# Moving the last weighing of a self-attention pair into the next pair's scores

## The chip, the cores and the metric

The kernel runs on one core of a Trainium2 chip. The metric is the device time of one execution in microseconds (us), taken as the median of several runs. The engines are named as the profile names them: PE is TensorE (matmul), PEld its weight loads, DVE is VectorE, ACT is ScalarE, POOL is GpSimd and SP is SyncE.

## What is computed

Two transformer blocks in float32 run over `x` (2 x 512 x 128) with a context of 2 x 154 x 96. The first block is a cross-attention of 16 heads of width 8 with a feed-forward. The second block, in which the change lies, is this:

```python
def _attn(xq, xc, Wq, Wk, Wv, Wo, bo):      # 16 heads of width 64
    q = (xq @ Wq).reshape(B, N, HEADS, D_HEAD)
    k = (xc @ Wk).reshape(B, S, HEADS, D_HEAD)
    v = (xc @ Wv).reshape(B, S, HEADS, D_HEAD)
    attn = softmax(einsum('bnhd,bshd->bhns', q, k) * scale)
    out = einsum('bhns,bshd->bnhd', attn, v).reshape(B, N, HEADS * D_HEAD)
    return out @ Wo + bo

x = _attn(_ln(x, g1, b1), _ln(x, g1, b1), Wq1, Wk1, Wv1, Wo1, bo1) + x   # self
x = _attn(_ln(x, g2, b2), context, Wq2, Wk2, Wv2, Wo2, bo2) + x          # cross
x = _geglu_ff(_ln(x, g3, b3), Wp, bp, Wf, bf) + x
```

## The kernel before

Each engine has one queue of instructions whose order is written out by hand, and semaphores join the queues. Self-attention is done by pairs of heads: 8 pairs for each of the 2 batches make pairs g = 0 to 15 (`NPAIR` = 16), and the cross-attention makes g = 16 to 31. For a self pair the 512 keys are cut into four chunks c = 0 to 3 of 128 keys.

For each self pair g, TensorE does the following, in this order (`attention`, L982 to L998):

1. `all_scores(g)` (L931) calls `scores(g, c)` for the four chunks. One unit of scores is eight matmuls into a two-bank tile `ST`: for each of the two heads three products of queries and keys split in fp32r (L749), and one that subtracts the rows' maxima (L751). A head stands in 64 of the array's 128 rows, so the two heads run side by side. Between them stand two matmuls of the maxima of pair g + 1 (`head_max`, L722), each into a bank `M`.
2. `side_before(g)` (work of other parts, at some g: the feed-forward of the first block at g = 3, values at g = 6 to 11, the spreading of inverse sums at g = 12).
3. `project(g + 2)`, the queries and keys of a later pair (L688 to L706), and `turn_pair(g + 1)`, which turns the maxima (L735).
4. `side_behind(g)` (more of the other parts), and for g >= 1 `denominators(g - 1)`, which is matmuls only for every second pair (L795).
5. `weigh(g, c)` for c = 0 to 3 (L767, matmuls at L780): the exponentials of chunk c, in fp32, as the moving operand against 64 columns of `V` for each head. All four accumulate in the bank `PV`. The profile records each as four matmuls, two for each head, and the heads run side by side in 64 columns each.

There are two `ST` tiles. `claim` (L315) gives them out in turn, and waits until the tile's last user is done: a unit of scores needs the exponential of two units before. There are also two banks `M`; a maximum waits until VectorE has read the one of two before (`maxima`, L1692, reductions at L1698).

ScalarE does for each pair (`attention`, L1371): `weighted(g - 1)` (L1356, a copy of `PV` to `AT` at L1361, which waits for the pair's last weighing), the four `exponentials(g, c)` (L1353) into `PT1[g % 2, c]`, then copies of the side work, then `leading(g + 2)` (L1339). VectorE does the eight reductions of the maxima of g + 1, then `maxima_rows(g + 1)` (L1711), `trailing(g + 2)` (L1685) and its side work. GpSimd adds the four chunks of exponentials (L1196, L1200). `weigh(g, 0)` waits for the copy of the pair before, since `PV` is one bank.

Of the kernel before, what the change touches and what calls it, by code (L numbers as in the profile page):

```python
# [11 lines left out]
TB = N // P  # L12
# [11 lines left out]
NPAIR = B * H // 2  # L24
# [19 lines left out]
def build(nc, a, out):  # L44
    ctx = ExitStack()
    with ctx:
# [138 lines left out]
        def pair(g):  # L185

            ph = self_att if g < NPAIR else cross_att
            return ph, g - ph.first

        def maxima_units(g):  # L190

            return range(TB if g < NPAIR else 2)

        VALUES = {6: (0, TB), 7: (0, TB + 2), 8: (1, 0), 9: (1, 1), 10: (1, 2), 11: (1, 3)}
        SPREADS = {9: (None, 0), 10: (None, 1), 11: (None, 2), 12: (3, None), 18: (None, 0), 19: (1, 2), 20: (3, None),
# [40 lines left out]
        def bank(key):  # L236
            return ST[ring[key]]
# [10 lines left out]
        def head(h):  # L248
            return slice(HD * h, HD * (h + 1))
# [61 lines left out]
        def _(pe):  # L311
# [3 lines left out]
            def claim(key, freed, count):  # L315

                k = len(s_uses)
                if k >= 2:
                    pe.wait_ge(*s_uses[k - 2])
                s_uses.append((freed, count))  # L320
                ring[key] = k % 2
                return ST[k % 2]
# [386 lines left out]
            def project(g):  # L709

                project_leading(g)
                project_trailing(g)

            def head_max(g, c, h):

                ph, i = pair(g)
                if c == 0 and h == 0:
                    pe.wait_ge(ph.hi, i + 1)
                r = R[:, g % 3, 0]
                m = claim_m()  # L720
                for qt, at in ((c, 0),) if ph is self_att else ((2 * c, 0), (2 * c + 1, S)):
                    ins = pe.matmul(m[:, at:at + ph.NK], r[head(h), 0, qt * P:(qt + 1) * P], r[head(h), 1, 0:ph.NK],  # L722
                                    start=True, stop=True)
                ins.then_inc(m_full, 1)
# [12 lines left out]
            def scores(g, c, unit=None, at=(4, 4)):  # L737

                ph, i = pair(g)
                u = claim(("st", g, c), ph.exp, ph.units * i + c + 1)
                k = slice(c * ph.KC, (c + 1) * ph.KC)

                def product(n, h):

                    if n < 3:
                        part_k, part_q = ((0, 0), (0, 1), (1, 0))[n]
                        return pe.matmul(u[0:ph.KC, h, :], R[head(h), g % 3, part_k, 1, k], R[head(h), g % 3, part_q, 0, :],  # L749
                                         start=(n == 0), stop=False)  # L750
                    return pe.matmul(u[0:ph.KC, h, :], onesr[head(h), 0:ph.KC], mrows[head(h), g % 2, :], start=False, stop=True)  # L751

                for n in range(5 if unit is not None else 4):
                    for h in range(2):
                        if unit is not None and n == at[h]:
                            head_max(g + 1, unit, h)
                            continue
                        part = n - (unit is not None and n > at[h])
                        if c == 0 and part == 0:
                            pe.wait_ge(ph.lo, i + 1)  # L760
                        if c == 0 and part == 3:
                            pe.wait_ge(mrow_set, g + 1)
                        ins = product(part, h)
                        if part == 3:
                            ins.then_inc(ph.st, 1)
# [165 lines left out]
            def all_scores(g):  # L931

                ph, i = pair(g)
                if g + 1 == NG:
                    beside = {}
                elif ph is cross_att:
                    beside = {0: (0, (0, 0)), 1: (1, (0, 1))}
                elif g + 1 == NPAIR:
                    beside = {0: (0, (0, 0)), 2: (1, (0, 0))}
                else:  # L940
                    beside = {0: (0, (0, 3)), 1: (1, (1, 3)), 2: (2, (2, 4)), 3: (3, (2, 4))}
                for c in range(ph.units):
                    scores(g, c, *beside.get(c, ()))

            def side_before(g):

                if g == 3:
                    hidden(1)
                if g in VALUES:
                    n, t = VALUES[g]  # L950
                    if n == 1:
                        loaded("wv2")
                    values(n, t)
                if g in SPREADS and SPREADS[g][0] is not None:
                    spread_inverse(g // 8 - 1, SPREADS[g][0])
                if g == 30:
                    turn(3, 0, False)
# [24 lines left out]
            def attention():  # L982

                start_attention()
                for g in range(NG - 1):
                    all_scores(g)
                    side_before(g)
                    if g + 2 < NG:
                        project(g + 2)
                    turn_pair(g + 1)  # L990
                    side_behind(g)
                    if g >= 1:
                        denominators(g - 1)
                    for c in range(pair(g)[0].units):
                        weigh(g, c)
                    if g == 21:
                        turn(2, 1, False)
                all_scores(NG - 1)  # L998
# [217 lines left out]
        def _(act):  # L1216
# [128 lines left out]
            def exponentials(g, c):  # L1345

                ph, i = pair(g)
                act.wait_ge(ph.st, 2 * (ph.units * i + c + 1))
                if g >= 2 and c == 0:
                    old, o = pair(g - 2)  # L1350
                    act.wait_ge(old.pv, o + 1)
                    act.wait_ge(old.sum, o + 1)
                act.activation(PT1[0:ph.KC, g % 2, c], bank(("st", g, c))[0:ph.KC, :, :],  # L1353
                               ACT.Exp, scale=HD ** -0.5).then_inc(ph.exp, 1)

            def weighted(g):  # L1356

                ph, i = pair(g)
                act.wait_ge(ph.pv, i + 1)
                b, j = i // PAIRS, i % PAIRS  # L1360
                act.activation(AT[:, j, b * N:(b + 1) * N], PV[:, :], ACT.Copy).then_inc(ph.pvs, 1)  # L1361
# [9 lines left out]
            def attention():  # L1371

                leading(0)
                values(0, 0)
                values(0, 1)
                exponentials0(7, 0, 1)
                values(0, 2)
                exponentials0(7, 2)
                values(0, 3)
                copy_half0(1, 1)  # L1380
                leading(1)
                for g in range(NG):
                    ph, i = pair(g)
                    if g == 22:
                        scale_features(2, 1)
                    if g >= 1 and g != 22:
                        weighted(g - 1)
                    if g == 2:
                        root(0, 1)
                    for c in range(ph.units):  # L1390
                        exponentials(g, c)
                    if g == 22:
                        weighted(g - 1)
                    if g == 3:
                        act.preload_act_table_set("gelu_and_others")
                        gelus(1)
                    if g in VALUES:
                        values(*VALUES[g])
                    if g == 30:
                        scale_features(3, 0)  # L1400
                    if g + 2 < NG:
                        leading(g + 2)
                    if g == 0:
                        values_bias0(1)
                    if g == 2:
                        scale_features(0, 1)
                    if g == 4:
                        root(1, 1)
                    if g == 5:
                        scale_features(1, 1)  # L1410
                    if g in (6, 7):
                        values(0, VALUES[g][1] + 1)
                    if g in (8, 16, 24):
                        inverse_guess(g // 8 - 1)
                    if g == 12:
                        leading_weights("q2", Wv, w12[:, :])
                    if g == 23:
                        leading_weights("wp", Wk, wp)
                    if g in (12, 20):
                        root(2, g // 8 - 1)  # L1420
                    if g == 13:
                        scale_features(2, 0)
                    if g == 28:
                        root(3, 0)
# [504 lines left out]
```

## Time and profile before

| | us |
|---|---|
| median of 3 runs | 459.2 (458.36 to 459.84) |
| the profiled execution, its own time | 462.21 |
| its span in the trace | 460.4 |
| PE busy | 443.2 (96%) |
| DVE busy | 277.1 (60%) |
| ACT busy | 238.9 (52%) |
| POOL busy | 214.5 (47%) |
| share of PE in the chain that ended last | 86% |

The self pairs take from about 96 us (the scores of pair 0) to about 305 us of the span. The granted TensorE clock is at full speed in that whole stretch. A busy PE is not a PE at its peak, as matmuls are pipelined and the recorded ends of neighbours overlap; how close it is to its bound is read from the starts of its instructions.

### The profile page before, as it was taken

The page shows a single profiled execution, that of the slowest core. Times are in us where ns is not written, and L with a number is a line of the kernel's source. Part 1 is how long each engine was busy: PE and PEld are TensorE (multiplying, and loading weights), DVE is VectorE, ACT ScalarE, POOL GpSimd, SP SyncE. Part 2 cuts the span into 40 slices and gives each one's busy share as a digit, 9 for nine tenths or more (in the row PEclk, how much of TensorE's full clock was granted, in tenths as well). Part 3 has the DMA queues.
Part 4 walks back from the last instruction along what each step waited for, and adds up shares of the span by engine and source line. Part 5 has one row for each costly group of instructions (what it writes and reads, how often), then busy time and mean ns, then how long its engine had stood idle before and what let it go on. Part 6 is the DMA issues. An engine that isn't in the chain of part 4 may idle for free.

```text
span 460.4 us, 7023 instructions
## 1 busy us (share of the span) xinstructions
PE 443.2 (96%) x2758; PEld 263.4 (57%) x2758; DVE 277.1 (60%) x511; ACT 238.9 (52%) x324; POOL 214.5 (47%) x186
## 2 busy tenths in 40 slices
PE   7999999989999999999999999999999999999896
PEld 3654665555655656655545765545575454754696
DVE  1766737576863576467656848447735577553753
ACT  2855465455557366555445526456326665237633
POOL 5488101026884796444566636873326444255010
PEclk9999899899999999999999999999999999999999
DMA  8600000000000100000001010020001000000000
GB/s 251 210 1 2 1 1 0 1 0 1 0 1 1 36 1 0 0 1 1 1 1 46 2 34 1 2 68 1 0 5 44 0 2 2 0 1 1 0 18 30
DMA packets 7985, 8.89 MB, mean 19 GB/s; under 512 B 561, under 2 KB 6129, under 8 KB 7953
## 3 DMA queue, kind: packets, MB, share of 16 engines
q1 hardware_dynamic: 7952, 8.45, 6.0%
q8 instruction: 22, 0.36, 0.3%
q14 instruction: 11, 0.08, 0.1%
HBM read 7.92 MB, written 0.52 MB: 18 GB/s over the span
## 4 chain that ended last, share of the span: by engine, by line
PE 86%; DVE 6%; ACT 4%; issue 2%; DMA 1%; SPq 0%
PE PV L780 18%; PE ST L749 14%; PE M L722 7%; PE ST L751 5%; PE M L828 5%; PE ST L688 5%; PE ST L650 4%; PE DEN L795 3%; ACT PT L1353 2%; PE ST L704 2%; PE ST L668 2%; PE ST L544 2%; PE ST L691 2%; PE M L870 2%; PE ST L366 1%
## 5 line engine op out<-in xcount | busy, mean ns | idle before, releaser
L1196 POOL TENSOR_TENSOR psums<-PT 128x1024 f32<-128x1024 f32 (+1 forms) x32 | 76.1, 2379 | 137.2 <-ACT PT L1353 137.1
L1353 ACT ACTIVATE PT<-ST 128x1024 f32<-128x1024 f32 (+1 forms) x96 | 98.0, 1024 | 39.6 <-PE ST L751 37.9
L1698 DVE TENSOR_REDUCE maxw<-M 128x1 f32<-128x512 f32 x128 | 83.6, 687 | 37.2 <-PE M L722 36.7
L749 PE MATMUL ST<-R 64*128 64x512 f32 (+1 forms) x576 | 105.4, 405 | 0.0
L780 PE MATMUL PV<-PT,V 128*64 128x512 f32 (+1 forms) x384 | 89.5, 601 | 0.0
L1200 POOL TENSOR_TENSOR psums<-psums,PT 128x1024 f32<-128x1024 f32 x32 | 75.9, 2373 | 2.5
L722 PE MATMUL M<-R 64*128 64x512 f32 (+1 forms) x256 | 72.0, 363 | 1.9 <-DVE maxw L1698 0.8
L749 PEld LDWEIGHTS ST<-R 64*128 64x128 f32 (+1 forms) x576 | 57.8, 171 | 14.2 <-ACT PT L1353 8.0
L722 PEld LDWEIGHTS M<-R 64*128 64x128 f32 x256 | 37.2, 185 | 38.1 <-issue 27.1
L780 PEld LDWEIGHTS PV<-PT,V 128*64 128x64 f32 (+1 forms) x384 | 24.7, 136 | 53.9 <-issue 51.5
L1361 ACT ACTIVATE AT<-PV 128x512 f32<-128x512 f32 x32 | 19.1, 598 | 62.5 <-PE PV L780 62.5
L751 PE MATMUL ST<-mrows,onesr 64*128 64x512 f32 (+1 forms) x192 | 47.3, 391 | 0.2 <-DVE mrows L1711 0.2
L1711 DVE TENSOR_TENSOR mrows<-M,cols 128x512 fp32r<-128x512 f32 x32 | 22.1, 691 | 40.5 <-PE M L735 40.5
L1701 DVE TENSOR_REDUCE maxw<-M 128x2 f32<-128x308 f32 x64 | 27.7, 474 | 23.2 <-PE M L722 23.2
L1159 POOL TENSOR_TENSOR X<-X,rows 128x128 f32<-128x128 f32 x24 | 10.4, 461 | 39.3 <-DVE xnT L1611 39.2
L751 PEld LDWEIGHTS ST<-mrows,onesr 64*128 64x128 f32 (+1 forms) x192 | 24.6, 170 | 4.3 <-DVE mrows L1711 0.7
L1339 ACT ACTIVATE R<-ST 128x1024 fp32r<-128x1024 f32 x16 | 16.4, 1024 | 11.2 <-PE ST L706 11.2
L1685 DVE TENSOR_TENSOR R<-ST,R 128x1024 fp32r<-128x1024 f32 x16 | 19.6, 1223 | 4.3 <-ACT R L1339 4.3
L828 PE MATMUL M<-Wo,AT 128*128 128x128 f32 x192 | 21.9, 275 | 0.0
L828 PEld LDWEIGHTS M<-Wo,AT 128*128 128x128 f32 x192 | 21.7, 192 | 0.3
L1556 DVE TENSOR_REDUCE maxw<-ST 128x4 f32<-128x616 f32 x20 | 15.2, 798 | 7.9 <-PE ST L399 7.9
L1311 ACT ACTIVATE lnv<-mv 128x4 f32<-128x4 f32 x7 | 1.4, 204 | 35.4 <-DVE mv L1597 35.4
(257 smaller groups left out, 677.0 us busy)
## 6 DMA issues: line engine op xcount, KB each, us to landing
Wo<-in_wo SPq DMA_DIRECT2D x2, 512.0 KB, 6.4
xnT<-in_xT SPq DMA_DIRECT2D x2, 256.0 KB, 3.4
psums<-in_sel SPq DMA_DIRECT2D x1, 512.0 KB, 5.2
X<-in_x SPq DMA_DIRECT2D x1, 512.0 KB, 6.5
w<-in_w SPq DMA_DIRECT2D x2, 256.0 KB, 6.8
PT<-in_wq SPq DMA_DIRECT2D x1, 512.0 KB, 7.8
PT<-in_wk SPq DMA_DIRECT2D x1, 512.0 KB, 8.1
PT<-in_wv SPq DMA_DIRECT2D x1, 512.0 KB, 7.8
```

The source lines that it names most:

```text
L688: pe.matmul(u[:, 0, :], wq[:, v, k], xh[:, n], start=(v == 0), stop=False)
L722: ins = pe.matmul(m[:, at:at + ph.NK], r[head(h), 0, qt * P:(qt + 1) * P], r[head(h), 1, 0:ph.NK], start=True, stop=True)
L749: return pe.matmul(u[0:ph.KC, h, :], R[head(h), g % 3, part_k, 1, k], R[head(h), g % 3, part_q, 0, :], start=(n == 0), stop=False)
L751: return pe.matmul(u[0:ph.KC, h, :], onesr[head(h), 0:ph.KC], mrows[head(h), g % 2, :], start=False, stop=True)
L780: ins = pe.matmul(PV[head(h), :], V[0:ph.KC, b * ph.NC + c, (2 * j + h) * HD:(2 * j + h + 1) * HD], PT1[0:ph.KC, g % 2, c, h, :], start=(c ...
L828: ins = pe.matmul(u[:, t * P:(t + 1) * P], AT[:, j, (TB * b + t) * P:(TB * b + t + 1) * P], Wo[:, j, :], start=(j == 0), stop=(j == PAIRS ...
L1196: ins = pool.tensor_tensor(s, p[:, 0], p[:, 1], ALU.add)
L1200: ins = pool.tensor_tensor(s, s, p[:, c], ALU.add)
L1353: act.activation(PT1[0:ph.KC, g % 2, c], bank(("st", g, c))[0:ph.KC, :, :], ACT.Exp, scale=HD ** -0.5).then_inc(ph.exp, 1)
L1698: ins = dve.tensor_reduce(maxw[:, g % 2, 0, at:at + 1], m[:, :], AX, ALU.max, negate=True)
L1701: ins = dve.tensor_reduce(maxw[:, g % 2, 0, at:at + 32:16], m[:, 0:2 * S].rearrange("p (t k) -> p t k", t=2), AX, ALU.max, negate=True)
L1711: dve.tensor_tensor(mrows[:, g % 2, :].rearrange("p (t n) -> p t n", t=TB), half_bank(("turn", g))[:, 0:P].unsqueeze(1).to_broadcast([P, T ...
```

## The change

For pairs g = 0 to 14 the weighing of chunk 3 leaves its place behind `weigh(g, 2)` and stands behind unit 1 of the scores of pair g + 1. ScalarE's copy of the pair's values stands behind the exponential of chunk 2 of pair g + 1, where it stood ahead of the exponential of chunk 0. Pair 15 and the cross pairs are left as they were. No instruction is added or taken away. The whole diff:

```diff
@@ -190,6 +190,10 @@
         def maxima_units(g):
 
             return range(TB if g < NPAIR else 2)
+
+        def late_weighing(g):
+
+            return 0 <= g < NPAIR - 1
 
@@ -941,6 +945,8 @@
                 for c in range(ph.units):
                     scores(g, c, *beside.get(c, ()))
+                    if c == 1 and late_weighing(g - 1):
+                        weigh(g - 1, TB - 1)
 
@@ -991,7 +997,7 @@
                     if g >= 1:
                         denominators(g - 1)
-                    for c in range(pair(g)[0].units):
+                    for c in range(pair(g)[0].units - late_weighing(g)):
                         weigh(g, c)
@@ -1383,12 +1389,14 @@
-                    if g >= 1 and g != 22:
+                    if g >= 1 and g != 22 and not late_weighing(g - 1):
                         weighted(g - 1)
                     if g == 2:
                         root(0, 1)
                     for c in range(ph.units):
                         exponentials(g, c)
+                        if c == 2 and late_weighing(g - 1):
+                            weighted(g - 1)
```

## Rows read from the trace of the kernel before

**Rows 1.** The waits: engine, line, releaser: us in total, times, longest

```profile
PEld ST L749 <- ACT PT L1353: 8.0, 28, 0.4
```

**Rows 2.** Timeline of PE, scores of pair 8 (start, us, engine, line)

```profile
199.46 1.03 PE L780 MATMUL PV<-PT,V 128*64 128x512 f32 x4
200.42 0.50 PE L722 MATMUL M<-R 64*128 64x512 f32 x1
...
202.62 0.52 PE L751 MATMUL ST<-mrows,onesr 64*128 64x512 f32 x2
203.00 0.73 PE L749 MATMUL ST<-R 64*128 64x512 f32 x4
...
205.34 0.50 PE L722 MATMUL M<-R 64*128 64x512 f32 x1
205.76 0.65 PE L668 MATMUL ST<-w,ctxT 96*77 96x512 f32 x1
```

**Rows 3.** Timeline of ACT, the same stretch: the copy, the third and fourth exponentials

```profile
200.54 0.60 ACT L1361 ACTIVATE AT<-PV 128x512 f32<-128x512 f32 x1 [2.57 <-PE PV L780]
...
204.45 1.03 ACT L1353 ACTIVATE PT<-ST 128x1024 f32<-128x1024 f32 x1 [0.25 <-PE ST L751]
205.73 1.02 ACT L1353 ACTIVATE PT<-ST 128x1024 f32<-128x1024 f32 x1 [0.26 <-PE ST L751]
```

**Rows 4.** Timeline of DVE, the same stretch: the eight reductions, merged by four

```profile
200.96 2.68 DVE L1698 TENSOR_REDUCE maxw<-M 128x1 f32<-128x512 f32 x4 [3.21 <-PE M L722]
...
203.99 2.57 DVE L1698 TENSOR_REDUCE maxw<-M 128x1 f32<-128x512 f32 x4 [0.35 <-PE M L722]
```

**Rows 5.** The chain in order of time: a matmul; weighings of a self and a cross pair

```profile
114.90 0.23 PE ST L704
...
116.36 3.58 PE PV L780 x16
...
309.92 1.87 PE PV L780 x8
```

**Rows 6.** Timeline of PE: scores' last maximum of pair 6; one weighing

```profile
177.70 0.39 PE L722 MATMUL M<-R 64*128 64x512 f32 x1
183.47 1.08 PE L780 MATMUL PV<-PT,V 128*64 128x512 f32 x4
```

**Rows 7.** Windows: the scores of pairs 2, 6, 9 and 15 (stretch, length, busy)

```profile
119.88:125.22 5.34, 5.34 (x42) 3.74 (x41) 4.55 (x8) 3.99 (x7) 3.86 (x8) 1.00 0.00 0
172.51:178.02 5.51, 5.46 (x42) 3.90 (x41) 5.19 (x8) 3.68 (x4) 1.85 (x2) 1.00 0.00 0
213.71:219.04 5.33, 5.33 (x42) 3.71 (x41) 4.94 (x8) 3.72 (x5) 1.48 (x1) 1.00 0.00 0
295.10:300.22 5.12, 4.67 (x42) 3.33 (x41) 1.73 (x4) 3.62 (x5) 3.23 (x5) 1.00 0.01 3
```

**Rows 8.** Timeline of PE, scores of pair 15: end of the second unit, start of the third

```profile
297.04 0.39 PE L751 MATMUL ST<-mrows,onesr 64*128 64x512 f32 x2
297.66 0.45 PE L722 MATMUL M<-R 64*128 64x154 f32 x4 [0.23 <-ACT PT L1353]
```

**Rows 9.** Timeline of ACT and PE around the feed-forward of pair 3

```profile
138.30 1.28 ACT L1395 ACT_TABLE_LOAD   x1
...
140.91 0.50 PE L688 MATMUL ST<-xh,Wq 128*128 128x512 f32 x1
```

**Rows 10.** Timeline of PE: the projection of pair 12, behind its spreading

```profile
259.42 0.73 PE L688 MATMUL ST<-xh,Wq 128*128 128x512 f32 x2 [0.31 <-ACT PT L1353]
```

**Rows 11.** Timeline of DVE: last work before the reductions in pairs 2 and 9

```profile
119.82 0.17 DVE L1597 TENSOR_SCALAR mv<-mv 128x4 f32<-128x4 f32 x1
...
213.47 0.75 DVE L1726 SCALAR_TENSOR_TENSOR recw<-recw,cols,work 128x512 fp32r<-128x512 f32 x1
```

**Rows 12.** Timeline of POOL and DVE ahead of pair 6

```profile
168.20 4.81 POOL L1200 TENSOR_TENSOR psums<-psums,PT 128x1024 f32<-128x1024 f32 x2
...
170.88 2.68 DVE L1671 TENSOR_TENSOR xl<-xnT,xh 128x512 fp32r<-128x512 f32 x1
```

## The prediction

> **What bounds the kernel now.** I read the page first. PE is busy for 96% of the span and holds 86% of the chain that ended last (the table ahead). Only work taken off PE, or idle time inside it, can shorten this kernel. Next come the waits. The one that touches the scores is short: 8.0 us in 28 waits for an exponential, over the whole program [rows 1]. It is a wait of the weight loads, and a load may wait while the array still works. So the third view is the timeline of PE in one pair, read by the starts. Pair 8 stands for the pattern, since 13 of the 16 self pairs have a score block between 5.33 and 5.37 us long ([rows 7] has pairs 2 and 9; pair 6 takes 5.51, pair 15 5.12, pair 0 more).
>
> In pair 8 the block runs from 200.42 to 205.76 [rows 2]. Its second unit ends with L751 at 202.62 + 0.52 = 203.14, and the third unit starts at 203.00. No time is lost there: the change puts the weighing into a place where PE already works through. The block's end has two bounds. The third exponential ends at 204.45 + 1.03 = 205.48 and frees the tile for the next user [rows 3]. The four reductions run from 203.99 in steps of 2.57 / 4 = 0.64, so the second of them ends at about 205.27, and only then can the last maximum start, at 205.34 [rows 2, 4]. The next work follows at 205.76. VectorE therefore paces the end of the block, counted from the start of the third unit: 205.76 - 203.00 = 2.76 us.
>
> **What the change removes.** Four weighings take 3.58 us, two take 1.87 [rows 5], so one takes (3.58 - 1.87) / 2 = 0.86 us at the end of a row of them. Fifteen go: 15 x 0.86 = 12.9 us off PE.
>
> **What it adds.** The same weighing, alone between two units of scores, costs more than 0.86. Wherever PE passes from the scores (64 rows of the array for each head) to a matmul over all rows, or back, the next start comes 0.07 us before the recorded end of the last one, and not earlier: 199.46 + 1.03 = 200.49 against 200.42; 205.34 + 0.50 = 205.84 against 205.76 [rows 2]; 177.70 + 0.39 = 178.09 against 178.02 [rows 6, 7]. Within a shape, matmuls follow each other every 0.23 us [rows 5] while a record lasts 0.39 [rows 6]. So a pass drains what is under way. At the new place L751 ends at 203.14, and the weighing can start at 203.07. A single weighing lasts 1.08 from its start to its recorded end [rows 6], so the scores go on 1.01 later, at 204.08. That is 204.08 - 203.00 = 1.08 us later than now.
>
> The Trainium skill says under TensorEngine Tiling (Array Packing), Key Properties, that changing the tiling mode, and not just the tile, drains the TensorE. The change has two mode changes more for each pair, and the trace agrees with that rule (0.39 to 0.50 us of the last record, less 0.07, in place of 0.23). A reader who took the weighing as 0.86 wherever it stands would get 0.22 less for each pair.
>
> From the third unit on all is paced from that unit's start: its maxima, their reductions, the last maximum 2.34 later, the next work 2.76 later. The wait for the second exponential in front of the fourth unit goes, but the last maximum waits for the same reduction as before, so this gives nothing back. The third exponential would end 203.00 + 1.08 + 2.48 = 206.56, before the block's new end at 205.76 + 1.08 = 206.84. The price is 1.08 in each block of pairs 1 to 14: 15.1 us. In pair 15 the cross maxima are short; its third unit starts at 297.66 after a wait of 0.23 for the exponential [rows 8]. The second unit ends at 297.04 + 0.39 = 297.43, so the scores go on at 297.36 + 1.01 = 298.37, 0.71 later; this block ends by its third exponential, so 0.71 stays.
>
> **ScalarE's copy.** It takes 0.60 [rows 3] and leaves a place where ACT idles (2.57 us of waiting in front of it), and where nothing waited for it: gain nothing. At the new place it stands between the third exponential and the fourth. In pair 8 the third ends at 206.56, the copy at 207.16, so the fourth ends at 207.16 + 1.03 = 208.19, where it ended at 206.75: 1.44 later, against 1.08 for PE. Who needs the fourth exponential? In most pairs the projection takes the tile of the third; the tile of the fourth is next claimed a stage later. Where values come first (pairs 6 to 11), the projection needs it, but 1.4 to 1.5 us of values lie in between. Two pairs have no cover. In pair 12 the projection waits for the fourth exponential already, with 0.31 [rows 10]. In pair 3 the table load at 138.30 follows it, and the projection at 140.91 waits for the gelus behind that [rows 9]. Each loses 1.44 - 1.08 = 0.36: together 0.7. Queued behind the copy is otherwise only `leading`, whose projection ends later than that. The copy is done before `weigh(g, 0)`, which stands behind the projection (at least 1.4 us). GpSimd's third and fourth adds are behind its own first at 2.4 us each, and cover the later exponentials.
>
> **What is late next.** The stretch between a projection and the next pair's scores loses 0.86, and VectorE's work there must still be done when the next maxima come. The first reduction is due 0.53 us after the block starts (200.96 against 200.42) [rows 2, 4]. In most pairs DVE is free over 0.6 us ahead of the block, so it is still in time. In pair 9 its work ends at 213.47 + 0.75 = 214.22, just when due [rows 7, 11]: it comes 0.86 late, which I take as 0.75 in the second unit. In pair 2 it ends at 119.99, 0.42 before it is due at 120.41: 0.44 late, taken as 0.3 (pair 6 is 0.45 late now, and is 0.17 longer [rows 7]). Together 1.05. Pairs 6 and 14 would lose 0.9 each in the same way, but there the last DVE work, L1671, lasts 2.68 because POOL's adds run until 168.20 + 4.81 = 173.01 [rows 12], and L1671 ends 0.55 behind them, at 173.56. The adds stand fixed to the exponentials, so L1671 ends where it did although it starts 1.08 later. I take nothing, and up to 1.8 for the upper end. By SBUF — State Buffer of the Trainium skill, in Who interferes with whom, the second of two such instructions blocks until the first is done; the trace shows just that.
>
> **The sum.** -12.9 + 15.1 + 0.7 (pair 15) + 0.7 + 1.05 = +4.7 us on the profiled execution of 462.2, whose median of plain runs is 459.2: I say **463.9 us**, 1.0% slower. A difference of 0.3%, 1.4 us, is about what a measurement here can tell from none.
>
> **The rivals.**
> 1. *The waits inside the scores are real idle time, and the weighing fills them: faster.* The waits last 8.0 / 28 = 0.29 us each [rows 1], and a block has two of them, 0.57. If PE idled in them, the weighing would cost 0.86 - 0.57 = 0.29 in a block, so 15 blocks would give 15 x 0.57 = 8.6; with 1.75 for the stragglers above that is 459.2 - 6.8 = 452.4. It decides as soon as more than 0.22 of a block's end is given back. Against it: the starts leave no gap at 203.00, and VectorE's pace hides what the fourth unit saves. For it: PE's recorded ends are modelled. Chance 0.12.
> 2. *A pass between the shapes costs nothing here.* Then the weighing costs 0.86 at either place, and only the stragglers of 1.75 stay, less 0.3 for the idle time of pair 15 that it fills: 459.2 + 1.45 = 460.7, at the edge of what can be told from none. Against it: the three passes above. Chance 0.14, which includes small givings back.
> 3. *The later fourth exponential or the late VectorE delays more pairs.* If the projections of pairs 6 to 11 also wait 0.36, that is 2.2 more; with pairs 6 and 14 late, 1.8 more: up to 467.9. It decides where a block ends within 0.36 of the tile it needs. Chance 0.12.
>
> **Chances and range.** The forecast holds 0.62. It has its own bounds: 0.93 to 1.19 for the middle weighing (entering by a record of 0.39 less what unit 2 overlaps, or by one of 0.50), so 461.8 to 465.5. The range of eight in ten takes in rival 2 and most of rival 3: 459.8 to 467.0. Faster by over 0.3%: 0.12. Within: 0.15. Slower by over 0.3%: 0.73.
>
> **What would show it.** PE's timeline of pair 8 should have three weighings at the end (2.72 us), a block of 6.4 us where it was 5.34, and inside it L780 starting 0.07 before the recorded end of L751 and 1.01 from there to the next L749. The last maximum should still stand 2.34 behind the start of the third unit. The projections of pairs 3 and 12 should lose more than others, and the reductions of pair 9 should start 1.4 us into its block. I am wrong if the block grows by under 0.86, or if the fourth exponential shows up as a releaser in the pairs 6 to 11.

## The result and the profile after

The changed kernel takes 463.94 us in the median (463.64 to 464.42) against 459.52 us for the kernel before in the same comparison (458.36 to 460.68). The ratio is 1.0106, with a 95% interval of 1.0085 to 1.0127: it is slower by 4.4 us, where the prediction said 4.7.

The busy shares of the engines tell nothing of that. The page after, its lines of busy time and of the chain by engine:

```profile
PE 444.2 (96%) x2758; PEld 261.4 (57%) x2758; DVE 274.9 (60%) x511; ACT 235.6 (51%) x324; POOL 215.6 (47%) x186
...
PE 84%; DVE 7%; ACT 6%; issue 2%; DMA 1%; SPq 0%
```

The two spans, 460.4 and 461.9 us, differ by less than the medians. Up to the end of pair 0's scores, ahead of the first late weighing, the execution of the kernel before was 3.3 us behind (102.62 against 99.33). Part of this is one more stretch in which PE's clock stood at its lower level (1.2 GHz), here as the windows view of the kernel before gives it (stretch, length, busy time and number of instructions of PE, PEld, DVE, ACT and POOL, then the granted clock as a share, and the DMA):

```profile
48.65:52.06 3.41, 3.41 (x17) 2.62 (x21) 1.27 (x4) 1.41 (x3) 0.00 (x0) 0.50 0.00 0
```

That stretch can explain at most half of its 3.41 us; what makes up the rest is not followed here. So the change is read in the stretch in which it lies, from there to the scores of the first cross pair. The windows view of the kernel before gives 202.45 us:

```profile
102.62:305.07 202.45, 201.64 (x1200) 115.38 (x1199) 126.17 (x196) 107.67 (x123) 128.29 (x81) 1.00 0.03 7
```

and that of the changed kernel 207.21, so the traces say +4.76 us:

```profile
99.33:306.54 207.21, 205.39 (x1200) 114.79 (x1199) 123.83 (x196) 104.45 (x123) 129.16 (x81) 1.00 0.03 7
```

Behind it both executions take the same: 155.35 and 155.36 us to the end.

PE's timeline in pair 8 of the changed kernel, around the new place and at the end of its block of scores (start, us, engine, line), is to be read beside [rows 2]:

```profile
201.09 0.52 PE L755 MATMUL ST<-mrows,onesr 64*128 64x512 f32 x2
201.55 1.08 PE L784 MATMUL PV<-PT,V 128*64 128x512 f32 x4
202.56 0.73 PE L753 MATMUL ST<-R 64*128 64x512 f32 x4
...
204.89 0.50 PE L726 MATMUL M<-R 64*128 64x512 f32 x1
205.32 0.66 PE L672 MATMUL ST<-w,ctxT 96*77 96x512 f32 x1
```

L755 ends at 201.61 and the weighing starts 0.06 before that. The scores go on 1.01 later, where a weighing among others takes 0.86. The last maximum (L726) starts 204.89 - 202.56 = 2.33 behind the third unit (2.34 before). The windows of the changed kernel show the parts of pair 8's block, the three weighings at home, and the whole blocks of pairs 2, 6, 9, 14 and 15 (to be read with [rows 7]):

```profile
198.90:201.55 2.65, 2.65 (x22) 1.90 (x21) 2.10 (x4) 1.02 (x1) 0.00 (x0) 1.00 0.00 0
201.55:202.56 1.01, 1.01 (x5) 0.20 (x5) 0.57 (x1) 0.90 (x1) 0.00 (x0) 1.00 0.00 0
202.56:205.32 2.76, 2.76 (x22) 1.90 (x21) 1.77 (x3) 1.42 (x3) 2.49 (x2) 1.00 0.00 0
209.68:212.41 2.73, 2.73 (x16) 0.77 (x13) 2.49 (x3) 1.25 (x3) 0.35 (x1) 1.00 0.00 0
...
115.90:122.55 6.65, 6.65 (x46) 3.92 (x45) 5.14 (x14) 3.76 (x6) 4.77 (x9) 1.00 0.00 0
169.69:177.11 7.42, 6.69 (x46) 3.92 (x45) 5.97 (x8) 3.35 (x4) 3.66 (x3) 1.00 0.00 0
212.41:219.48 7.07, 6.70 (x46) 3.93 (x45) 5.56 (x10) 3.37 (x4) 2.50 (x2) 1.00 0.01 2
284.46:290.88 6.42, 6.42 (x46) 4.00 (x45) 4.86 (x8) 3.36 (x4) 2.49 (x2) 1.00 0.00 0
295.87:301.69 5.82, 5.60 (x46) 3.54 (x45) 1.73 (x4) 3.02 (x4) 3.73 (x5) 1.00 0.01 3
```

Pair 8's block is 6.42 us, 1.07 more than before, and the row of three weighings at home, behind the projection, takes 2.73, 0.86 less. Ten other pairs have blocks like pair 8's, of 6.40 to 6.43. Pair 6's block stands out with 7.42, pair 9's with 7.07, pair 2's with 6.65.

### The profile page after: what moved, and what is told of

Same layout as the page of the kernel before. It is cut to its first block, busy times and chain, and to the rows that moved or that the text cites. A ratio compares the mean times of both kernels' runs of the same rounds, so it can differ in the third digit from the quotient of the medians.

```text
span 461.9 us, 7023 instructions
## 1 busy us (share of the span) xinstructions
PE 444.2 (96%) x2758; PEld 261.4 (57%) x2758; DVE 274.9 (60%) x511; ACT 235.6 (51%) x324; POOL 215.6 (47%) x186
## 4 chain that ended last, share of the span: by engine, by line
PE 84%; DVE 7%; ACT 6%; issue 2%; DMA 1%; SPq 0%
PE PV L784 18%; PE ST L753 14%; PE M L726 7%; PE M L832 5%; PE ST L755 5%; PE ST L692 5%; PE ST L654 4%; PE DEN L799 3%; ACT PT L1359 2%; PE ST L708 2%; PE ST L672 2%; PE ST L695 2%; PE M L874 2%; DVE maxw L1564 1%; PE ST L370 1%
## 5 line engine op out<-in xcount | busy, mean ns | idle before, releaser
L784 PE MATMUL PV<-PT,V 128*64 128x512 f32 (+1 forms) x384 | 92.8, 605 | 0.0
L726 PE MATMUL M<-R 64*128 64x512 f32 (+1 forms) x256 | 73.3, 368 | 2.8 <-DVE maxw L1706 1.9
L726 PEld LDWEIGHTS M<-R 64*128 64x128 f32 x256 | 37.2, 185 | 41.5 <-issue 27.1
L784 PEld LDWEIGHTS PV<-PT,V 128*64 128x64 f32 (+1 forms) x384 | 23.4, 136 | 50.9 <-issue 43.7
L755 PE MATMUL ST<-mrows,onesr 64*128 64x512 f32 (+1 forms) x192 | 47.4, 391 | 0.2 <-DVE mrows L1719 0.2
L755 PEld LDWEIGHTS ST<-mrows,onesr 64*128 64x128 f32 (+1 forms) x192 | 24.6, 170 | 4.4 <-DVE mrows L1719 0.7
```

The costliest lines, as they stand in the source:

```text
L784: ins = pe.matmul(PV[head(h), :], V[0:ph.KC, b * ph.NC + c, (2 * j + h) * HD:(2 * j + h + 1) * HD], PT1[0:ph.KC, g % 2, c, h, :], start=(c ...
```

## The experiments

"Self stage" below is the stretch from the end of pair 0's scores to the first cross scores, 202.45 us before and 207.21 with the change. Each is read from the run's own trace, where it is free of what happens ahead of it. A "late" weighing stands in or behind the next pair's scores, one "at home" where the kernel before has it. A "shape" is the part of the array that a matmul takes: 64 or all rows, 64 columns or the full width. Each ratio is against the kernel before in the same comparison.

### Does leaving the scores' shape cost time, or only the work?

Two kernels add one small matmul to the kernel before, between units 1 and 2 of the scores. They differ only in the rows that it covers:

```diff
                     scores(g, c, *beside.get(c, ()))
+                    if c == 1 and 1 <= g < NPAIR:
+                        pe.wait_ge(self_att.pvs, g)
+                        pe.matmul(PV[:, 0:32], ident[0:P, :], ident[0:P, 0:32], start=True, stop=True)
```

> The kernel before, with one fp32 matmul of 32 columns over all 128 rows added between units 1 and 2 of the scores of pairs 1 to 15, into the bank of the values, which is then free; its result is overwritten by the weighings. My theory (leaving the shape of 64 rows and coming back drains the array each time): 0.3 to 0.5 us in each of 15 blocks, 4.5 to 7.5 us over before. Rival (a change of shape costs nothing, only the matmul's own time does): the same as its twin over 64 rows, within 0.05 us in each block.

The twin has `0:HD` (64 rows) in place of `0:P`.

> The twin of the kernel with the small matmul over all rows: the same fp32 matmul of 32 columns at the same place, but over rows 0 to 63, the shape that the scores have, so that the shape never changes. My theory: 0.05 to 0.2 us in each block, 0.8 to 3 us over before, and at least 0.2 us in each block less than the twin. Rival (a change of shape costs nothing): as the twin, within 0.05 us in each block.

Measured: over all rows 465.65 us against 458.98, ratio 1.0142 (1.0102 to 1.0183); over 64 rows 459.17, ratio 1.0008 (0.9989 to 1.0028). Pair 8's block in the windows view, all rows first, then 64 rows:

```profile
199.58:205.32 5.74, 5.74 (x44) 4.12 (x43) 4.44 (x7) 3.70 (x5) 1.89 (x1) 1.00 0.00 0
```

```profile
196.84:202.19 5.35, 5.35 (x44) 3.98 (x43) 4.45 (x7) 3.71 (x5) 1.50 (x1) 1.00 0.00 0
```

PE's timelines around the small matmul (L946), in the same order:

```profile
201.78 0.52 PE L751 MATMUL ST<-mrows,onesr 64*128 64x512 f32 x2
202.22 0.41 PE L946 MATMUL PV<-ident 128*128 128x32 f32 x2
202.56 0.72 PE L749 MATMUL ST<-R 64*128 64x512 f32 x4
```

```profile
199.04 0.52 PE L751 MATMUL ST<-mrows,onesr 64*128 64x512 f32 x2
199.27 0.30 PE L946 MATMUL PV<-ident 64*128 64x32 f32 x2
199.42 0.73 PE L749 MATMUL ST<-R 64*128 64x512 f32 x4
```

The matmul over 64 rows starts while L751 runs, and the next unit 0.15 later. It costs nothing, where 0.05 to 0.2 a block was expected: the starts before hold about that much room ahead of the third unit. (Pair 6 alone is 0.18 longer; the self stage is 202.52 us, 0.07 over before.) The same matmul over all rows starts only 0.08 before L751's recorded end and holds the next unit for 0.34. With equal data type, columns and place, the block grows by 0.4 for the shape alone, and the self stage takes 207.99, 5.5 over before. The Trainium skill says in TensorEngine Tiling (Array Packing), Key Properties, that a change of the tiling mode, and not just of the tile, drains the TensorE; this pair of traces agrees.

### Is the price one for the place, or one for each weighing?

Two weighings stand at the new place, and two at home:

```diff
                     if c == 1 and late_weighing(g - 1):
+                        weigh(g - 1, TB - 2)
                         weigh(g - 1, TB - 1)
...
-                    for c in range(pair(g)[0].units - late_weighing(g)):
+                    for c in range(pair(g)[0].units - 2 * late_weighing(g)):
```

> The changed kernel with two late weighings, of chunks 2 and 3, side by side at the new place, and two left at home. My theory (the place has a fixed price for two changes of shape, a weighing beside another costs 0.86 wherever it stands): the weighings in the block last 1.01 + 0.86 = 1.87 us and the blocks 7.27; home gives 0.86 back again, so the pairs without late VectorE work are no slower than with one. VectorE's work comes later still ahead of pairs 2, 6 and 9 (0.86 each) and now ahead of 4, 10 and 12 (about 0.4 each): 3.8 us more than the changed kernel, 467.7. Rival (each late weighing has its own price of 1.07): blocks of 7.5, and 3 us more than that, 470 or over.

Measured: 468.19 us, ratio 1.0194 (1.0153 to 1.0235). Pair 8's block, and PE inside it:

```profile
202.42:209.69 7.28, 7.28 (x50) 4.29 (x49) 4.43 (x7) 3.36 (x4) 2.52 (x2) 1.00 0.00 0
```

```profile
205.06 1.94 PE L784 MATMUL PV<-PT,V 128*64 128x512 f32 x8
206.93 0.50 PE L753 MATMUL ST<-R 64*128 64x512 f32 x2
```

The two weighings last 206.93 - 205.06 = 1.87 us, and the block 7.28: 0.86 more than with one. The second late weighing takes what it gives back at home. The price of 0.2 us belongs to the place. The self stage took 213.15 us, 5.9 more than with the change, but this execution had a stretch of 3.41 us at PE's lower clock (1.2 GHz), nearly all of it in the two late weighings inside pair 6's scores, which lasted 3.53 in place of 1.87:

```profile
175.31:178.72 3.41, 3.41 (x10) 0.58 (x10) 0.44 (x1) 1.00 (x1) 2.33 (x1) 0.50 0.00 0
```

Less these 1.66 it is 4.3 more; 3.8 was expected. Most of the difference is pair 14, whose block is 7.80, 0.5 longer than pair 8's, and for which nothing late had been counted.

### Where else could the weighing stand?

Behind unit 2:

```diff
-                    if c == 1 and late_weighing(g - 1):
+                    if c == 2 and late_weighing(g - 1):
                         weigh(g - 1, TB - 1)
...
-                        if c == 2 and late_weighing(g - 1):
+                        if c == 3 and late_weighing(g - 1):
                             weighted(g - 1)
```

> The late weighing stands behind unit 2 of the next scores, and the copy behind the fourth exponential. My theory (two changes of shape cost the same at any place, but VectorE paces the last unit only where the third unit follows its two reductions closely): the fourth unit starts 1.11 us later, and no longer waits for the reductions, which gives 0.16 back: blocks of 6.29 (5.34 before, 6.41 with the change), 3.1 us over before in all. Rival (the place makes no difference): blocks of 6.4 and 4.4 to 4.8 us over before.

Measured: 463.84 us, ratio 1.0092 (1.0071 to 1.0112); self stage 206.61, 4.16 over before. Its PE timeline in pair 8 has the end of the third unit, the weighing, and the block's end:

```profile
201.88 0.39 PE L726 MATMUL M<-R 64*128 64x512 f32 x1
202.20 1.08 PE L784 MATMUL PV<-PT,V 128*64 128x512 f32 x4
203.21 0.74 PE L753 MATMUL ST<-R 64*128 64x512 f32 x4
...
204.26 0.39 PE L726 MATMUL M<-R 64*128 64x512 f32 x1
204.59 0.65 PE L672 MATMUL ST<-w,ctxT 96*77 96x512 f32 x1
```

The block took 6.31, as expected; the self stage did not, as 3.1 over before was expected. In the block the fourth unit's last maximum no longer waits for a reduction, its record is 0.39 in place of 0.50, and the next work starts 0.33 after it in place of 0.43. The sum was too low mainly because the copy behind the fourth exponential has no cover in two pairs. In pair 15 PE now waits for it with the first weighing at home, and the stretch to the next scores is 0.53 longer. Pair 3's gelus (the feed-forward's activations on ScalarE) come 0.49 later behind the block than with the change:

```profile
302.18 1.08 PE L784 MATMUL PV<-PT,V 128*64 128x512 f32 x4 [0.45 <-ACT AT L1367]
```

Behind all four units, ahead of the projection (the same edit with `c == 3` for the weighing, the copy also behind the fourth exponential):

> The late weighing stands behind all four units of the next scores, ahead of the projection, so that it joins matmuls over all rows and no change of shape is added; the copy stands behind the fourth exponential. My theory: the weighing costs 0.92 us here against the 0.86 saved, and the late reductions of pairs 2, 6 and 9 stay (1.7 us): 2.6 us over before (ratio 1.006), score blocks of 5.34. Rival (weighing a pair late costs 0.3 us for a reason other than the shape, such as its own start or the wait for the bank): 4.4 us over before or more.

Measured: 461.60 us, ratio 1.0071 (1.0042 to 1.01); self stage 204.94, 2.49 over before. Pair 8's block of scores and the weighing behind it:

```profile
197.54:202.88 5.34, 5.34 (x42) 3.73 (x41) 4.43 (x7) 3.12 (x4) 1.48 (x1) 1.00 0.00 0
202.88:203.89 1.01, 1.01 (x5) 0.20 (x4) 0.80 (x2) 0.98 (x1) 0.93 (x2) 1.00 0.00 0
```

The total came as expected and its split did not. The weighing costs 1.01 here too, not 0.92: it uses the array as 128 rows by two times 64 columns, the work behind it uses 77 or 128 columns in one piece, and this is one pass more between shapes. It costs 0.15 a pair, against 0.22 inside the scores. I had looked at the rows alone. Four things made up for these 0.09 more a pair, 1.35 in all. Pair 12, whose projection waited for the fourth exponential anyway, is 0.47 cheaper than the other pairs, and pair 3 0.21. Pair 15's block is 0.29 shorter than before, as its projection waited for an exponential there. And the late reductions of pairs 2, 6 and 9 cost 1.3 and not 1.7.

### What do the late reductions cost?

The changed kernel, without the late weighings ahead of pairs 2, 6 and 9:

```diff
-            return 0 <= g < NPAIR - 1
+            return 0 <= g < NPAIR - 1 and g not in (1, 5, 8)
```

> The changed kernel, but pairs 1, 5 and 8 weigh at home, so that the blocks of pairs 2, 6 and 9, ahead of which VectorE has its last work late, keep their 0.86 us of cover. My theory: these three late weighings cost 0.21 us each for the place and 0.24, 0.83 and 0.64 us for late reductions, so 2.3 us come back: about 2.4 us over before (ratio 1.005). Rival (every late weighing costs the same 0.3 us): 0.95 us come back, 3.8 us over before (ratio 1.008).

Measured: 461.51 us, ratio 1.0036 (1.0011 to 1.0061); self stage 204.69. The three pairs are at 5.34 to 5.36 us, pair 6 even 0.17 under before:

```profile
115.98:121.33 5.34, 5.34 (x42) 3.73 (x41) 4.55 (x8) 4.00 (x7) 3.87 (x8) 1.00 0.00 0
169.33:174.67 5.34, 5.34 (x42) 3.70 (x41) 5.01 (x8) 3.68 (x4) 1.67 (x2) 1.00 0.00 0
210.83:216.19 5.36, 5.36 (x42) 3.75 (x41) 4.94 (x8) 3.70 (x5) 1.49 (x1) 1.00 0.00 0
```

2.5 us of 4.8 come back with 3 of 15 late weighings. They were the dear ones: with the change, pairs 2, 6 and 9 lose 0.24, 0.83 and 0.65 beside the price of the place.

Pair 6 had been expected to lose nothing. This kernel moves GpSimd's bias from ahead of its adds in pair 5 to behind them:

```diff
                 if g == 5:
                     normal(1, 1, X)
-                    add_bias(1, "bo1", 1)
...
                 ins.then_inc(ph.sum, 1)
+                if g == 5:
+                    add_bias(1, "bo1", 1)
```

> The changed kernel, with GpSimd's four additions of a bias to X (1.7 us) moved from ahead of its three adds of the exponentials of pair 5 to behind them. My theory (VectorE's subtraction L1671 ahead of pair 6 lasts 2.5 us since it stands beside those adds, and they are late since GpSimd had the bias ahead of them): the adds start 1.4 us or more earlier, the subtraction lasts at most 1.8 us, and the first half of pair 6's scores takes 2.64 to 2.9 us in place of 3.64: 0.7 to 0.9 us less than the changed kernel. Rival (the subtraction is late for another reason, its inputs): no change.

Measured: 463.36 us, ratio 1.0091 (1.0058 to 1.0123); one of the four executions took 2350.13 us and is not in the ratio. Self stage 206.22, 0.99 less than with the change. Its pair 6 has the block of the others:

```profile
169.97:176.39 6.42, 6.42 (x46) 4.00 (x45) 4.86 (x8) 3.36 (x4) 4.49 (x6) 1.00 0.00 0
```

GpSimd's adds and VectorE's subtraction ahead of pair 6, in the changed kernel (one answer for each engine):

```profile
166.06 4.81 POOL L1206 TENSOR_TENSOR psums<-psums,PT 128x1024 f32<-128x1024 f32 x2
...
168.92 2.50 DVE L1679 TENSOR_TENSOR xl<-xnT,xh 128x512 fp32r<-128x512 f32 x1
```

and with the bias behind:

```profile
165.01 4.83 POOL L1205 TENSOR_TENSOR psums<-psums,PT 128x1024 f32<-128x1024 f32 x2
...
169.19 1.20 DVE L1680 TENSOR_TENSOR xl<-xnT,xh 128x512 fp32r<-128x512 f32 x1
```

The subtraction ends 0.55 us behind the adds in both (171.42 against 170.87, 170.39 against 169.84), as in [rows 12]. Started at about the same place of its pair, it takes 2.50 or 1.20 by when GpSimd is done, though it reads nothing that the adds write. That VectorE waits for GpSimd there is what these rows show. SBUF — State Buffer of the Trainium skill says in Who interferes with whom that a VectorE instruction with two inputs in SBUF contends with a GpSimd instruction that reads SBUF.

### And ScalarE's copy?

The copy alone, all four weighings at home:

```diff
                     scores(g, c, *beside.get(c, ()))
-                    if c == 1 and late_weighing(g - 1):
-                        weigh(g - 1, TB - 1)
...
-                    for c in range(pair(g)[0].units - late_weighing(g)):
+                    for c in range(pair(g)[0].units):
```

> ScalarE's copy alone is moved behind the third exponential; the weighing stays at home with the three others. My theory (the weighing's own price at its new place, not the copy, makes the change slow): the fourth exponential ends about 0.5 us later, which shows only in the pairs 3 and 12, whose projections wait for it: 0.9 to 1.3 us over before (ratio 1.002 to 1.003), score blocks of 5.34 as before. Rival (the copy between two exponentials is what delays every pair): 3 us or more.

Measured: 459.24 us against 459.59, ratio 0.9991 (0.998 to 1.0001); self stage 202.72, 0.28 over before. ScalarE in pair 12 of this kernel:

```profile
252.96 1.03 ACT L1357 ACTIVATE PT<-ST 128x1024 f32<-128x1024 f32 x1 [0.26 <-PE ST L755]
253.89 0.59 ACT L1365 ACTIVATE AT<-PV 128x512 f32<-128x512 f32 x1
254.36 1.03 ACT L1357 ACTIVATE PT<-ST 128x1024 f32<-128x1024 f32 x1
```

From the third exponential to the fourth it is 1.40 us, where 1.28 passed before [rows 3]. Unhindered, the copy starts 0.93 after an exponential, and the next exponential 0.47 after the copy. The idle 0.26 ahead of each exponential takes in most of that. The copy costs 0.12, and not the 0.5 that I expected here, so the 0.9 to 1.3 us expected in all did not come either. What makes the change slow is not the copy.

The changed kernel with the copy behind the second exponential:

```diff
-                        if c == 2 and late_weighing(g - 1):
+                        if c == 1 and late_weighing(g - 1):
                             weighted(g - 1)
```

> The changed kernel, with the copy behind the second exponential, where ScalarE idles 1.3 us while the late weighing runs. My theory: the third exponential is not touched, the fourth ends where PE leaves it, and the projections of pairs 3 and 12 come 0.11 and 0.13 us earlier: 0.2 to 0.3 us less than the changed kernel, which the clock of a plain run can't tell. Rival (the copy delays more than that): over 1 us less.

Measured: 463.33 us, ratio 1.0087 (1.0054 to 1.0121); self stage 206.97, 0.24 less than with the change, as expected, of which pairs 3 and 12 hold 0.12 and 0.11.

### What the runs point to

Only pair 14's weighing stands late, and GpSimd's bias stands behind its adds:

```diff
-            return 0 <= g < NPAIR - 1
+            return g == NPAIR - 2
...
-                    add_bias(1, "bo1", 1)
...
+                if g == 5:
+                    add_bias(1, "bo1", 1)
```

> What the runs point to: only pair 14 weighs its last chunk late, into the scores of pair 15, which wait for exponentials (0.86 saved for 0.70), and GpSimd's bias of pair 5 stands behind its adds, so that pair 6 is not late (0.17). My theory: 0.33 us under before, less than a run can tell: ratio 0.9985 to 1.0005. Rival (a late weighing costs at pair 15 what it costs elsewhere): 0.2 us over before in the trace, as the sum of 0.2 for the place and 0.17 back.

Measured: 459.22 us against 459.49, ratio 0.9997 (0.9976 to 1.0017). Its blocks of pairs 6 and 15:

```profile
169.19:174.53 5.33, 5.33 (x42) 3.72 (x41) 4.96 (x8) 3.72 (x5) 3.67 (x6) 1.00 0.00 0
290.79:296.63 5.84, 5.62 (x46) 3.55 (x45) 1.73 (x4) 3.02 (x4) 4.81 (x6) 1.00 0.01 3
```

The self stage takes 202.11 us, 0.34 less than before, as worked out; the time can't tell it from none.

## Why the prediction was right, point by point

- **What is removed.** 0.86 us for each weighing at the end of a row. Measured 3.58 - 2.73 = 0.85 to 0.86. Right.
- **The lone weighing.** 1.08 more in a block was predicted, 1.07 measured. That the price over 0.86 is in the change of shape, and not in the weighing, is shown by the small matmuls (0.40 against nothing) and by the two late weighings (7.28 us).
- **VectorE paces the block's end.** The next work stands 2.76 behind the third unit with and without the change. Behind unit 2, where the weighing comes after both reductions were asked for, 0.1 us came back, so this pacing is worth 0.1. Right.
- **Pair 15.** 0.71 predicted, 5.82 - 5.12 = 0.70 measured.
- **Late VectorE work.** Pair 9 was 0.75, measured 0.65; pair 2 was 0.3, measured 0.24. In pair 9 the first reduction stands 213.69 - 212.41 = 1.28 into the block, where 1.4 was said:

```profile
213.03 0.75 DVE L1734 SCALAR_TENSOR_TENSOR recw<-recw,cols,work 128x512 fp32r<-128x512 f32 x1
213.69 0.68 DVE L1706 TENSOR_REDUCE maxw<-M 128x1 f32<-128x512 f32 x1
```

- **Pair 6: this step failed.** It said that GpSimd's adds stand fixed to the exponentials, so that the subtraction ends where it did. In pair 14 they do, and it cost nothing (block of 6.42). In pair 5 they stand behind GpSimd's normalisation and bias, which do not start from pair 5's exponentials: the first add starts 163.58 - 158.41 = 5.17 us behind the start of pair 5's scores, where it was 165.74 - 161.42 = 4.32. The subtraction ended that much later too, counted in the same way, and pair 6 lost 0.83 more than the place's price. I had this as a bound (0.9 each for pairs 6 and 14) and not as the value; the timeline of POOL one window earlier would have shown the bias in front of the adds, with no wait for an exponential between.
- **The fourth exponential: mis-sized.** It was said to come 1.44 later and to cost 0.36 in pairs 3 and 12. It came 1.20 later and cost 0.11 and 0.13. The recorded durations of neighbours on ScalarE overlap, as PE's do: 1.03 and 0.60 in the records, 0.93 and 0.47 from start to start.
- **The sum** was 4.7 against 4.76 in the traces. Part of that closeness is luck: 0.8 too little for pair 6 stands against 0.5 too much for the fourth exponentials and 0.2 for pairs 2 and 9, and the rest is rounding.
- **Rival 1**, that the waits in front of units 3 and 4 were idle time to be filled, is refuted by the middle block. Those waits were of weight loads, 0.29 us each. A little room there was, though, and the prediction's "no time is lost there" missed it: L751 starts at 202.62, matmuls of one shape follow every 0.23, and the third unit starts at 203.00 and not at 202.85 [rows 2]. By this estimate 0.15 us was free, as much as the small matmul over 64 rows used. The sum did not suffer, as it counted from 203.00. **Rival 2**, that a pass costs nothing, is refuted by the pair of small matmuls. Of **rival 3**, pair 6 came true, and the projections behind the values stayed on time within 0.05.

## What to carry over

Moving work on the bottleneck engine into "a wait" pays only if the engine's own starts show a gap there; waits of the weight loads don't. On TensorE a matmul of another shape between two of one shape has to wait for what is under way, and so has the next. Here a weighing cost 0.2 us more than in a row of its kind, and a tiny matmul 0.4 where its twin cost nothing. So work is best kept in runs of one shape, and a second piece at the same place is free of that price. And a stretch that gets shorter must be read for every engine that works in its cover: three pairs of fifteen made up over a third of this loss.

## What was not expected of the hardware

A shape of the same rows but other columns also counts. With the weighing behind all four units, the weighing (128 rows, twice 64 columns) starts at 109.18 in pair 1 and the projection (128 rows, 128 columns) at 110.19: 1.01 us, as inside the scores, and not 0.86. It is 1.01 in all 15 pairs. A size that does not split the array does not count: in pair 8 of that run, L692 (128 rows, 128 columns) starts 0.56 before the recorded end of L672 (96 rows, 77 columns):

```profile
203.89 1.94 PE L672 MATMUL ST<-w,ctxT 96*77 96x512 f32 x4
205.27 0.80 PE L692 MATMUL ST<-xh,Wq 128*128 128x512 f32 x1
```

And ScalarE starts the next instruction 0.10 to 0.12 us before the recorded end of the one before when nothing else holds it (0.93 of 1.03, 0.47 of 0.59).
